# A routed expert block whose last 64 up columns hold high and low part in one stationary operand

## The reference

```python
router = xf @ Wg                                   # xf: (8192, 256), 8 experts
top_logits, idx = jax.lax.top_k(router, 2)
probs = softmax(top_logits)                        # w: probs put at the chosen experts
h = silu(einsum('tc,ech->eth', xf, W1)) * einsum('tc,ech->eth', xf, W2)   # hidden width 352
y = einsum('eth,ehc,te->tc', h, W3, w)
hs = silu(xf @ Ws1) * (xf @ Ws2)                   # shared expert, hidden width 704
y = y + hs @ Ws3
```

## Time and profile before

| | |
|---|---|
| median of 3 runs | 2384.82 us (2382.97 to 2386.32) |
| span of the profiled execution, first to last instruction | 2353.9 us |
| what the median has beyond this span | 30.9 us |
| TensorE busy in the span | 2316.8 us (98%) |
| VectorE / ScalarE / GpSimd busy | 1978.7 (84%) / 1709.7 (73%) / 1012.1 (43%) |
| routed blocks | from about 1420 to 1920 us, one each 6.88 us |
| granted TensorE clock, mean | 0.999 |

### The profile page before, as it was taken

The page is one execution under the profiler, slowest core; times in us unless marked ns, Lnnn a source line. Parts: engine busy times, 40 slices in busy tenths (PEclk is TensorE's granted clock), DMA queues, the critical chain, the costliest instruction groups (busy, mean ns, idle before and its releaser), DMA issues.

```text
span 2353.9 us, 50539 instructions
## 1 busy us (share of the span) xinstructions
PE 2316.8 (98%) x19358; PEld 1543.2 (66%) x19358; DVE 1978.7 (84%) x2874; ACT 1709.7 (73%) x3276; POOL 1012.1 (43%) x1013
## 2 busy tenths in 40 slices
PE   7999999999999999999999999999999999999998
PEld 6875444444444444444444438999999989888998
DVE  7888999999999999999999966777777765555555
ACT  4447888888999999998999997777777753333332
POOL 2112556553225555454454334434343354455444
PEclk9999999999999999999999999999999999999999
DMA  8994544543224444343343335777777753344432
GB/s 295 375 338 173 169 155 161 165 145 99 81 83 131 125 123 136 114 128 118 121 127 109 108 96 192 241 240 236 242 236 247 233 174 108 108 129 125 123 108 90
DMA packets 189745, 383.07 MB, mean 163 GB/s; under 512 B 54164, under 2 KB 100756, under 8 KB 176292
## 3 DMA queue, kind: packets, MB, share of 16 engines
q1 hardware_dynamic: 151536, 219.17, 29.1%
q0 software_dynamic: 36880, 159.87, 21.3%
q10 hardware_dynamic: 1088, 0.79, 0.1%
HBM read 247.86 MB, written 140.31 MB: 165 GB/s over the span
## 4 chain that ended last, share of the span: by engine, by line
PE 65%; DVE 29%; issue 3%; ACT 2%; DMA 1%; SPq 0%; POOL 0%; DVEq 0%; POOLq 0%; ACTq 0%
PE ps L569 62%; DVE mx L1054 17%; DVE mx L1051 10%; PE ps L582 3%; DMA Md<-mT 1%; ACT ptb L889 0%; ACT pta L889 0%; ACT qkH L869 0%; DMA xr<-Xn 0%; DMA OPS<-Md 0%; DVE mT L1070 0%; SPq L1562 0%; DMA xt<-in_x 0%; DVE qkL L1041 0%; POOL rstd L1270 0%
## 5 line engine op out<-in xcount | busy, mean ns | idle before, releaser
L569 PE MATMUL ps<-OPS 54*128 54x512 f32 (+1 forms) x4096 | 734.7, 439 | 5.2 <-DMA OPS<-Md 2.4
L1054 DVE TENSOR_REDUCE mx<-ps 128x2 f32<-128x1024 f32 x620 | 734.2, 1216 | 5.7 <-PE ps L569 4.8
L569 PEld LDWEIGHTS ps<-OPS 54*128 54x128 f32 (+1 forms) x4096 | 366.3, 184 | 394.0 <-ACT pta L889 263.7
L889 ACT ACTIVATE pta<-ps 128x512 f32<-128x512 f32 x1024 | 549.7, 605 | 65.5 <-PE ps L569 56.8
L889 ACT ACTIVATE ptb<-ps 128x512 f32<-128x512 f32 x1024 | 544.9, 609 | 47.4 <-PE ps L569 38.8
L1051 DVE TENSOR_REDUCE mx<-ps 128x1 f32<-128x512 f32 x808 | 514.0, 677 | 2.1 <-PE ps L569 2.0
L569 PE MATMUL ps<-OPS,WB 128*128 128x256 f32 (+2 forms) x2364 | 384.5, 315 | 3.1 <-DVE VB L1181 1.5
L569 PEld LDWEIGHTS ps<-OPS,WB 128*128 128x128 f32 (+1 forms) x2364 | 332.3, 183 | 28.2 <-issue 3.9
L569 PE MATMUL ps<-pta,VB 128*32 128x192 f32 (+7 forms) x4520 | 324.7, 370 | 0.0
L569 PE MATMUL ps<-ptb,VB 128*32 128x512 f32 (+1 forms) x3064 | 296.9, 461 | 0.0
L1314 POOL TENSOR_SCALAR m<-m 128x16 f32<-128x16 f32 x64 | 16.9, 265 | 540.8 <-DVE m L1064 540.8
(11 more groups left out here) (172 smaller groups left out, 2867.5 us busy)
## 6 DMA issues: line engine op xcount, KB each, us to landing
OPS<-QKh SPq DMA_DIRECT2D x512, 64.0 KB
Xs<-zero POOLq DMA_DIRECT2D x71, 256.0 KB, 3.6
xr<-Xs SPq DMA_DIRECT2D x71, 256.0 KB, 5.3
Ys<-VB SPq DMA_DIRECT2D x71, 256.0 KB, 5.0
QKh<-qkH SPq DMA_DIRECT2D x16, 1024.0 KB, 7.3
QKl<-qkL SPq DMA_DIRECT2D x16, 1024.0 KB, 8.8
OPS<-QKl SPq DMA_DIRECT2D x256, 64.0 KB
asum<-Sd SPq DMA_DIRECT2D x64, 256.0 KB
```

What stands on the lines that cost most here:

```text
L569: return self.e.matmul(o, l, r, start=start, stop=stop)
L889: self.e.activation(pt(m)[:, half * GT:(half + 1) * GT], ps[:, score_bank(n), :], ACT.Exp).then_inc(sem["exp"], 1)
L1054: self.e.reduce_max(mx[:, r % 2, hh, i, :], ps[:, bank - 1:bank + 1, :], AX.X).then_inc(sem["mxred"], 2)
```

## The change

The third part of the hidden width has 96 gate columns and 96 up columns, 12 matmuls. The change regroups them. Up's last 32 columns are put behind the 352 gate columns in DRAM and in the weight tile, so that one stationary operand of 128 columns gives the 96 gate rows and 32 up rows (six matmuls). The other 64 up columns have high and low part side by side in a stationary operand of 128 columns: with the low part of the tokens it is one matmul, with the high part another, four for the two halves of the input dimension. Their result is 128 rows: rows 0 to 63 with the high weights, 64 to 127 with the low weights, which have to be added. ScalarE copies the lower rows to SBUF, VectorE adds the upper ones, and GpSimd multiplies with the Silu. VectorE multiplies the other 32. In place of one VectorE product there are a copy, an addition and two products, on three engines.

The new operand needs a new split: GpSimd casts these 64 x 2 columns itself and subtracts them, beside the first piece, which is 768 columns now instead of 704; the second piece is 512 instead of 704.

```diff
-W2_AT, W3_AT = 2 * HE, 4 * HE
-PIECES = ((0, W2_AT), (W2_AT, W3_AT), (W3_AT, RAW))
+W1C, W2C = HE + 32, 2 * P
+W2_AT = 2 * W1C
+W3_AT = W2_AT + 2 * W2C
+REST = W3_AT + 3 * D
+LO = REST + 4 * 64
+PIECES = ((0, W2_AT), (W2_AT, W3_AT), (W3_AT, REST))
...
 class Tensor
+            def up_rest(self, o, xh, xl, wt):
+                for c in range(2):
+                    both = wt[:, REST + c * P:REST + (c + 1) * P]
+                    self.mm(o, both, xl[:, c, :], c == 0, False)
+                    last = self.mm(o, both, xh[:, c, :], False, c == 1)
+                return last
...
-                self.mm3(ps[0:hn, bank, 0:BT], self.operands(xh, xl, wt, h0, hn))
-                self.mm3(ps[0:hn, bank, BT:2 * BT], self.operands(xh, xl, wt, W2_AT + h0, hn)).then_inc(sem["up"], 1)
+                self.mm3(ps[:, bank, 0:BT], self.operands(xh, xl, wt, h0, W1C))
+                if hc < 2:
+                    up = self.mm3(ps[:, bank, BT:2 * BT], self.operands(xh, xl, wt, W2_AT + h0, W2C))
+                else:
+                    up = self.up_rest(ps[:, bank, BT:2 * BT], xh, xl, wt)
+                up.then_inc(sem["up"], 1)
...
 class Scalar, block_up
                 self.w.wait_ge("up", n + 1)
+                if hc == 2:
+                    self.e.copy(hfq[0:64, k, :], ps[64:P, bank, BT:2 * BT]).then_inc(sem["ulo"], 1)
                 self.e.activation(sgq[0:hn, k, :], ps[0:hn, bank, 0:BT], ACT.Silu).then_inc(sem["sg"], 1)
                 if b or hc:
                     self.split_block(b + 1, hc)
                 self.w.wait_ge("down", (n - 8) // 3 + 1)
+                if hc == 2:
+                    self.w.wait_ge("up2", b + 1)
                 self.w.wait_ge("hf", n + 1)
...
 class Vector, block_up
+                else:
+                    self.w.wait_ge("ulo", b + 1)
+                    self.w.wait_ge("sg", n + 1)
+                    e.tensor_tensor(hfq[0:64, k, :], ps[0:64, bank, BT:2 * BT], hfq[0:64, k, :], ALU.add
+                                    ).then_inc(sem["us"], 1)
+                    e.tensor_tensor(hfq[64:96, k, :], ps[96:P, bank, 0:BT], sgq[64:96, k, :], ALU.mult
+                                    ).then_inc(sem["hf"], 1)
...
 class Pool, pack_expert: 7 DMAs for an expert in place of 5
+                e.dma_start(gate[:, :, HE:W1C], rows(w2[:, W2C + 64:HE])).then_inc(sem["wd"], 16)
+                e.dma_start(d[:, REST:RAW].rearrange("p (c n) -> p c n", c=2), rows(w2[:, W2C:W2C + 64])
+                            ).then_inc(sem["wd"], 16)
...
 class Pool, split_block
+                if b < NBLK:
+                    rest = wt[:, REST:LO].rearrange("p (c u n) -> p c u n", c=2, u=2)
+                    raw = WR[b % 3][:, REST:RAW].rearrange("p (c n) -> p c n", c=2)
+                    self.e.tensor_copy(rest[:, :, 0, :], raw).then_inc(sem["wsr"], 1)
+                low = self.e.tensor_tensor(wt[:, LO + lo:LO + hi], WR[b % 3][:, lo:hi], wt[:, lo:hi].bitcast(F32),
+                                           ALU.subtract)
+                if b < NBLK:
+                    self.w.wait_ge("wsr", b + 1)
+                    low = self.e.tensor_tensor(rest[:, :, 1, :], raw, rest[:, :, 0, :].bitcast(F32), ALU.subtract)
+                low.then_inc(sem["wslp"], 1)
...
 class Pool, block_up
+                if hc == 2:
+                    k = (3 * b + hc) % 4
+                    self.w.wait_ge("sg", 3 * b + hc + 1)
+                    self.w.wait_ge("us", b + 1)
+                    self.e.tensor_tensor(hfq[0:64, k, :], hfq[0:64, k, :], sgq[0:64, k, :], ALU.mult
+                                         ).then_inc(sem["up2"], 1)
```

More of the change, by code:

```diff
@@ L71 @@
     "xt qkmm vmm mxmm smm pv obmm rtmm sct gmm up down sdn "
-    "wsplh woh xh qkh vev exp acc1 rte rtc wsh sch sg hh yev och "
-    "wspll bq wol ob st ag ve norm xl qkl mxred m16 mtr rcp rt rtw wslv scl hf hl ocl s1 gf fin "
-    "nhalf rstd lgc pad vcp ones zmem mng mnh mnl nrm rg rtd rtm rtp rtb rts wslp xb ya"
+    "ulo wsplh woh xh qkh vev exp acc1 rte rtc wsh sch sg hh yev och "
+    "us wspll bq wol ob st ag ve norm xl qkl mxred m16 mtr rcp rt rtw wslv scl hf hl ocl s1 gf fin "
+    "up2 wsr nhalf rstd lgc pad vcp ones zmem mng mnh mnl nrm rg rtd rtm rtp rtb rts wslp xb ya"
 ).split()
@@ L917, in split_block @@
                     self.w.wait_ge("zero", 16 * NBLK)
-                    self.w.wait_ge("wd", 80 * NE)
+                    self.w.wait_ge("wd", 112 * NE)
                 self.e.copy(WB[b % 3][:, lo:hi], WR[b % 3][:, lo:hi]).then_inc(sem["wsh"], 1)
@@ L930, in block_up @@
                 self.w.wait_ge("hf", n - 3)
+                if hc == 2:
+                    self.w.wait_ge("hl", n - 3)
+                    self.w.wait_ge("hh", n - 3)
                 self.w.wait_ge("up", n + 1)
+                if hc == 2:
+                    self.e.copy(hfq[0:64, k, :], ps[64:P, bank, BT:2 * BT]).then_inc(sem["ulo"], 1)
                 self.e.activation(sgq[0:hn, k, :], ps[0:hn, bank, 0:BT], ACT.Silu).then_inc(sem["sg"], 1)
@@ L1336, in pack_expert @@
                 d = Wd[x * P:(x + 1) * P, :]
-                e.dma_start(d[:, 0:W2_AT].rearrange("p (c n) -> p c n", c=2), rows(w1)).then_inc(sem["wd"], 16)
-                e.dma_start(d[:, W2_AT:W3_AT].rearrange("p (c n) -> p c n", c=2), rows(w2)).then_inc(sem["wd"], 16)
+                gate = d[:, 0:W2_AT].rearrange("p (c n) -> p c n", c=2)
+                e.dma_start(gate[:, :, 0:HE], rows(w1)).then_inc(sem["wd"], 16)
+                e.dma_start(gate[:, :, HE:W1C], rows(w2[:, W2C + 64:HE])).then_inc(sem["wd"], 16)
+                e.dma_start(d[:, W2_AT:W3_AT].rearrange("p (c n) -> p c n", c=2), rows(w2[:, 0:W2C])
+                            ).then_inc(sem["wd"], 16)
+                e.dma_start(d[:, REST:RAW].rearrange("p (c n) -> p c n", c=2), rows(w2[:, W2C:W2C + 64])
+                            ).then_inc(sem["wd"], 16)
                 e.dma_start(d[:, W3_AT:W3_AT + 2 * D].rearrange("p (c n) -> p c n", c=2), rows(w3[0:2 * P, :])
                             ).then_inc(sem["wd"], 16)
-                e.dma_start(d[0:96, W3_AT + 2 * D:RAW], w3[2 * P:HE, :]).then_inc(sem["wd"], 16)
+                e.dma_start(d[0:96, W3_AT + 2 * D:REST], w3[2 * P:HE, :]).then_inc(sem["wd"], 16)
                 self.w.wait_ge("zmem", 1)
-                e.dma_start(d[96:P, W3_AT + 2 * D:RAW], zero[0:32, :]).then_inc(sem["wd"], 16)
+                e.dma_start(d[96:P, W3_AT + 2 * D:REST], zero[0:32, :]).then_inc(sem["wd"], 16)
             def route(self, i):
```

29 lines of the change are left out of this document (14 added, 15 removed).

## The result

The changed kernel takes 2496.57 us (median of 4 runs, 2492.49 to 2497.90), the kernel before 2383.89 on the same chip (4 runs): ratio 1.0475, 95% interval 1.0461 to 1.0490. It is 112.7 us slower; 2441 was predicted, and the range ended at 2468. The direction was right, the size half of what came.

The account below looks back on a forecast made before the run. TensorE bounds the kernel at 6.88 us a block; afterwards the helpers' loop would, at 7.65. Span 2353.9 + 54 + 2 = 2410, plus 30.9 from span to run median, gives 2441 us; range 2390 to 2468.

Parts of the forecast that it names:

- the loop of the three helpers: Routed blocks: the cycle through ScalarE, VectorE and GpSimd sets the pace afterwards, 7.65 us a block instead of 6.88.
- the wait for the port: VectorE's two-SBUF-input subtraction and GpSimd's operations exclude each other on shared ports; VectorE waits for the running one's end.
- The wider operand: Third part's matmuls: 128 stationary columns cost no more than 96, 0.118 us each.
- Durations of the new operations: Each block's added work: GpSimd product 0.72, cast 0.25, subtractions 1.85 and 0.44; ScalarE copy 0.38 us.
- Subtraction 1.85 less 0.13, until VectorE's blocked subtraction gets the port, 1.72; that one 0.33: Loop step: VectorE's 128x256 subtraction starts 0.13 before GpSimd's big subtraction's recorded end; its next operation 0.33 later.
- The gather stands behind the product: GpSimd's queue: the weight gather issued after the new product still lands with 1.8 us of cover, costing nothing.
- Starts one behind the other: Loop distances start to start, such as copy to Silu 0.28, Silu to addition 0.48, addition to product 0.49 us.
- The start of the stage, 2 us: Routed stage's start: GpSimd's pending power operation delays block 0's product and shifts first blocks, 0 to 4 us, 2 taken.
- Rival C: Third part: VectorE's low split takes the port before GpSimd's product; some 8.6 us a block, +120, 2507 us; chance 5%.
- Rival B: Routed blocks: VectorE and GpSimd do not hold each other up, TensorE stays the bound at 6.64; 2368 us; chance 14%.
- Rival A: VectorE's 128x256 subtraction gets the port before GpSimd's big one; 7.0 to 7.2 a block, about 2401 us; chance 20%.
- the likeliest case: Whole kernel: helpers' loop at 7.65 us a block, 2441 us, own range 2425 to 2462; chance 57%.

Follow-up runs that it names:

- two_more_matmuls: Changed kernel with two more 256-column matmuls in each third part, their result overwritten, so TensorE does as many as before: 2472.43 us, ratio 1.0470 to before.
- reordered_late_wait: Changed kernel with helper steps reordered, 64-column split on VectorE, gather earlier, TensorE's second-weight-piece and down waits later: 2369.10 us, ratio 0.9948 to before.
- gather_first: Changed kernel with GpSimd issuing the weight gather ahead of its product instead of behind it: 2433.67 us, ratio 1.0286 to 1.0322 to before.
- product_on_vector: Changed kernel with the 64x256 product done by VectorE instead of GpSimd: 2433.04 us, ratio 1.0285 to 1.0323 to before.
- before_again: Kernel before the change, nothing altered, run and profiled once more on another chip: 2383.55 us, profiled span 2381.7.
- small_first_gather_first: Changed kernel with GpSimd's small subtraction ahead of its big one and the gather issued ahead of its product: 2379.54 us, ratio 1.0068 to 1.0099 to before.
- before_reordered: Kernel before the change with VectorE's low parts moved, next tokens cast first, and the second weight piece awaited only ahead of up: 2383.31 us, ratio 1.0004.
- added_wait: Changed kernel with one more wait: GpSimd awaits its big subtraction's end before issuing the small one: 2446.63 us, ratio 1.0344 to 1.0391 to before.

## Why the prediction was wrong

The mechanism was right: the loop of the three helpers sets the pace and TensorE's saving is worth nothing. Terms of the sum were mis-sized, the wait for the port most of all. Step by step:

- **The wider operand, TensorE's 0.237 a block, and that it would be worth nothing:** right for this kernel. The ten matmuls start 0.12 apart, 1.20 us for all, and two_more_matmuls costs nothing. Where TensorE does set the pace, in reordered_late_wait, 0.15 of the 0.237 came.
- **Durations of the new operations:** right. The product 0.72 (predicted 0.72), the small subtraction 0.46 (0.44), the big one 1.84 (1.85), GpSimd's cast 0.25 to the next (0.25), ScalarE's copy 0.37 (0.38).
- **"Subtraction 1.85 less 0.13, until VectorE's blocked subtraction gets the port, 1.72; that one 0.33":** this step failed. I let VectorE have the port at the end of the operation that it met, and left out the next operation of the same burst, though it stood in my list of the order. The measured step is 2.48 instead of 2.05. What I relied on was the earlier trace rows, in which VectorE did get in between two GpSimd operations. That occurs as well, in gather_first and product_on_vector in the blocks all through the stage, where GpSimd had paused ahead of its cast. 0.43 in each of 64 blocks is 28 of the 56 us between 2441 and 2497.
- **"The gather stands behind the product" at nothing:** the landing was indeed no matter (no wait for it in the blocks), but I looked only at the DMA and not at the issuing engine. The issue begins while VectorE's low split has 0.66 left and takes 1.53 us instead of 0.96; GpSimd's cast starts 0.17 later, 11 us in all. The trace that I predicted from has this too, at 1431.74 (1.43) and 1442.01 (1.51).
- **Starts one behind the other:** ScalarE's copy out of partitions 64 to 127 does not overlap its neighbours, 0.23 for both sides; the addition on VectorE and the hand-over to GpSimd are 0.10 slower; the product's way back is 0.02 faster. 20 us. With the two above it is 59 us, 3 more than are missing: the first three distances between stores, 24.9 us in all beside 29.3 in before_again, did not grow by 0.77 each as the sum has it.
- **The start of the stage, 2 us:** not separable; 5 us of the difference between spans lie ahead of the first store, where two executions of the kernel before are 23 us apart.
- **Rival C** is near the measured time (2507) but is not what came: the product is served first (0.72, and the low split behind it has 1.19). **Rival B** failed by the port, as argued. **Rival A** is near what small_first_gather_first makes of the kernel: 7.20 and 20 us over before, within the 10 to 24 that it was given.
- **What the changed profile would show:** TensorE's idle time is 1.41 and not 0.8 to 1.0, VectorE's 128x256 subtraction has 2.42 and not 1.9, its low split of 768 columns 1.19 and not 1.4, GpSimd is busy 4.78 a block and not 4.3. As said are the wait of ScalarE for the product (0.73) and the absence of a wait for the weights.
- **The range:** my ends for the likeliest case moved durations only. The uncertain thing was who is served at the port, and I had it in one place (rival A) and one direction, downward. The same question one operation later goes the other way and was worth 28 us.

That gather_first and product_on_vector both take the kernel from 112 to 73 us over before shows how much hung on this; 0.44 of the 0.6 that each gains in a block is the port. By the earlier trace rows VectorE's subtraction already waited 0.9 us in each block before the change, without costing anything; before_reordered takes the wait away (VectorE busy 269 us of 400 instead of 316) and gains nothing.

The Trainium skill, "SBUF — State Buffer", section "SBUF: two separate sides", says that whichever of the two starts first gets the pair for the whole instruction, and the other blocks. The trace agrees for a single pair of instructions. For a series it does not say enough: in the changed kernel the operation that started later was served first, 1714.62 before a subtraction that had been waiting from 1712.95.

## What to carry to other kernels

Where an edit takes work from the engine that sets the pace, sum the loop of the engines that feed it, start to start, with the slack it has now; here 0.77 us of slack met 1.54 of new steps by the prediction and 2.45 by the trace (8.56 less 6.11), and shares of busy time (GpSimd 39%) said nothing of it. An operation of VectorE with two inputs in SBUF that meets a burst of GpSimd operations can have to wait for more of them than the one it met; it is to be priced both ways, and should stand where nobody waits for what is queued behind it. When such a loop is found, reorder before undoing: the same work with its low parts and waits moved went from 112 us slower to 13 us faster than before.

## What was not expected of the hardware

- GpSimd can keep the port from one operation to the next over a waiting VectorE subtraction (2.42 us in 64 blocks of the changed kernel). It did not where it had paused ahead of the burst (1.82 in gather_first, 1.76 in product_on_vector) or where the next operation has to wait for the end of the one before (2.00 in added_wait), nor in two blocks of the changed kernel without a pause (2.35, 2.60). What in the engine decides it is open.
- The issue of an indirect DMA by GpSimd is held up by a VectorE subtraction with two SBUF inputs that is running when it begins: 0.96 us with 0.13 left, 1.28 with 0.40, 1.53 with 0.66. Those that begin after it cost it nothing (1.02 in before_reordered). In "SBUF — State Buffer", section "Who interferes with whom", the Trainium skill holds it for inferred that such an operation leaves the making of descriptors alone. The direct DMAs that GpSimd issues behind the routed blocks (L1488) agree: in the changed kernel two that began with 0.87 of such a subtraction left took 0.82 and 0.77, and 0.72 to 0.78 is what the others took. What the indirect one has beyond them is that it reads its indices from a tile in SBUF (widx); that this reading is what waits is argued, not shown.
- Two operations that the change brings, whose input and output start at different partitions, do not overlap with their neighbours: ScalarE's copy at 1708.68 starts 0.02 after the end of the one before, and VectorE's 32x256 product at 1710.03 starts 0.03 after it, where most others start 0.08 to 0.10 before that end. That the shift is the cause isn't shown: VectorE's product at 1712.05 in the same block has none, and starts 0.03 after the subtraction ahead of it (1711.61 + 0.41).
